# A decoder layer on one core: attention's last periods and the start of the feed forward placed in one order

## What is computed

```
x = x + SelfAttention(LayerNorm(x))        # causal, 16 heads of 64
x = x + CrossAttention(LayerNorm(x), ctx)  # 64 context rows a batch, one head, mask by key
x = x + FFN(LayerNorm(x))
FFN(x): h = silu(x w1 s1) * (x w2 s2); h = gelu(h h1 ..); h = gelu(h h2 ..); h w3 s3
# w1, w2: 256 -> 1024; h1, h2: 1024 -> 1024; w3: 1024 -> 256
```

## Time and profile before

| | us |
|---|---|
| median of 3 runs (lowest to highest) | 1719.96 (1719.22 to 1722.33) |
| the profiled execution | 1718.95 |
| its span, from first to last instruction | 1717.1 |
| PE busy in the span | 1594.4 (93%) |
| DVE busy | 1118.2 (65%) |
| ACT busy | 968.8 (56%) |
| POOL busy | 496.6 (29%) |

### The profile page before, as it was taken

The page is one execution under the profiler, slowest core; times in us unless marked ns, Lnnn a source line. Parts: engine busy times, 40 slices in busy tenths (PEclk is TensorE's granted clock), DMA queues, the critical chain, the costliest instruction groups (busy, mean ns, idle before and its releaser), DMA issues.

```text
span 1717.1 us, 26314 instructions
## 1 busy us (share of the span) xinstructions
PE 1594.4 (93%) x9398; PEld 1332.2 (78%) x9398; DVE 1118.2 (65%) x2733; ACT 968.8 (56%) x2220; POOL 496.6 (29%) x802
## 2 busy tenths in 40 slices
PE   4999999999999999999974489999999899999998
PEld 3788888888888888888863378778888678888887
DVE  5888888888888888888866735665445343333433
ACT  4778777787777877878753334434444342222222
POOL 1444444444444444444440301010001011111110
PEclk9999999999999999999996599999999999999999
DMA  3000000000000000000003312333111352222221
GB/s 135 1 1 1 25 2 26 1 1 26 1 26 1 1 26 2 13 1 2 13 13 138 110 62 75 110 112 111 69 62 44 135 184 75 75 74 74 74 95 41
DMA packets 55470, 87.50 MB, mean 51 GB/s; under 512 B 4128, under 2 KB 33184, under 8 KB 55328
## 3 DMA queue, kind: packets, MB, share of 16 engines
q1 hardware_dynamic: 55328, 85.62, 14.7%
HBM read 56.25 MB, written 29.36 MB: 50 GB/s over the span
## 4 chain that ended last, share of the span: by engine, by line
PE 78%; DVE 11%; ACT 3%; issue 3%; DMA 2%; POOL 2%; SPq 0%; DVEq 0%; ACTq 0%; POOLq 0%
PE bank L913 13%; PE bank L915 11%; PE bank L365 9%; PE bank L380 8%; PE bank L352 7%; PE bank L300 7%; PE bank L302 6%; PE bank L301 6%; PE bank L919 2%; DVE gt L1272 1%; PE bank L1003 1%; DVE Hb L1153 1%; DVE P L606 1%; PE bank L1004 1%; ACT Hb L1048 1%
## 5 line engine op out<-in xcount | busy, mean ns | idle before, releaser
L693 POOL TENSOR_SCALAR P<-P,stats 128x512 f32<-128x512 f32 (+3 forms) x512 | 263.1, 537 | 255.2 <-DVE stats L616 253.6
L470 ACT ACTIVATE P<-P,stats 128x512 f32<-128x512 f32 (+3 forms) x512 | 284.2, 558 | 4.1 <-DVE stats L606 2.0
L521 DVE TENSOR_TENSOR PT<-bank,PT 128x512 fp32r<-128x512 f32 (+1 forms) x384 | 228.8, 596 | 31.7 <-ACT PT L428 31.6
L606 DVE CUSTOM_DVE_ANT_0 P<-bank,cmask 128x384 f32<-128x384 f32 (+3 forms) x512 | 236.2, 481 | 5.6
L428 ACT ACTIVATE PT<-bank 128x512 fp32r<-128x512 f32 (+1 forms) x384 | 194.7, 524 | 66.6 <-PE bank L365 54.1
L1153 DVE TENSOR_TENSOR Hb<-gt,Hb 128x512 fp32r<-128x512 f32 x128 | 91.2, 712 | 212.9 <-ACT Hb L1048 195.1
L913 PE MATMUL bank<-Hb,hw 128*128 128x512 f32 x512 | 206.8, 404 | 6.9 <-POOL flag L1351 4.7
L913 PE MATMUL bank<-w,hw 128*128 128x512 f32 x512 | 203.7, 398 | 3.1 <-DVE w L1153 3.0
L365 PE MATMUL bank<-ident,P 128*128 128x128 f32 x1280 | 190.9, 279 | 6.6 <-DVE PT L521 4.5
L380 PE MATMUL bank<-PT,V 128*128 128x512 f32 (+3 forms) x1024 | 182.8, 321 | 0.0
L380 PEld LDWEIGHTS bank<-PT,V 128*128 128x128 f32 x1024 | 166.8, 188 | 16.1
(11 more groups left out here) (201 smaller groups left out, 3290.3 us busy)
## 6 DMA issues: line engine op xcount, KB each, us to landing
h_scratch<-go SPq DMA_DIRECT2D x64, 256.0 KB, 2.0
xs<-x_scratch SPq DMA_DIRECT2D x24, 512.0 KB, 4.0
qf<-h_scratch SPq DMA_DIRECT2D x32, 256.0 KB, 4.0
pf<-h_scratch SPq DMA_DIRECT2D x32, 256.0 KB, 4.7
stg<-in_h SPq DMA_DIRECT2D x13, 512.0 KB, 3.7
x<-in_x SPq DMA_DIRECT2D x8, 512.0 KB, 4.0
x_scratch<-x SPq DMA_DIRECT2D x8, 512.0 KB, 2.9
x_scratch<-xs SPq DMA_DIRECT2D x8, 512.0 KB, 3.0
```

The lines of the kernel that those rows point to most:

```text
L470: e.activation(p, p, ACT.Exp, bias=st_[:, k:k + 1], scale=-1.0, accum_out=st_[:, 8 + k:9 + k]).then_inc(s_exp, 1)
L521: return e.tensor_tensor(dst, a, b.bitcast(f32), ALU.subtract)
L606: e.tensor_tensor_reduce(P_tile(P, i, a), Sbank(P, i, a)[:, 0:n], cmask[:, 512 - n:512], -1.0, 3.0e38, ALU.add, ALU.min, stats[P % 4][:, k ...
L693: e.tensor_scalar(p, p, stats[P % 4][:, k:k + 1], 1.0, ALU.mult, ALU.mult).then_inc(s_norm, 1)
```

## The change

The two halves become one order. `order()` writes all 68 periods, each engine's period cut in `start`, `mid` and `end`, and puts the early items of the rest between them. `attention_over` is gone. Every tile has a fixed address, those of the rest on top of attention tiles that are dead by then, and each first writer waits on the semaphore of the last reader (`tile_free` and `place_free`, and waits in the items). The item `ln` is cut in `lnsum`, `lnpow`, `lnnorm`; loading a piece (`load`), splitting it (`piece`) and taking its largest value (`big`) are items of their own; there are four staging tiles of 1024 columns in place of six. The splits of `h1` (pieces 10 to 16) and the largest values of pieces 9 to 16 stand between the eight w(0,m), then come `flag 0` and the layer norm of batch 1, which stood ahead of them.

```diff
+def order():
+    between = {
+        (53, 2): [("load", 0), ("load", 1)],
+        (56, 0): [("piece", 0), ("load", 2), ("load", 3), ("load", 4)],
+        (57, 0): [("piece", 1)],
+        (59, 2): [("x1store", 6), ("consts",)],
+        (62, 0): [("piece", 2), ("xload", 0), ("load", 5)],
+        (62, 1): [("piece", 3)],
+        (63, 0): [("xk", 0), ("xk", 1), ("lnsum", 0, 0)],
+        (63, 1): [("mask",), ("bq",), ("piece", 4), ("lnpow", 0, 0), ("lnnorm", 0, 0)],
+        (64, 0): [("xf", 0), ("xf", 1), ("xc",), ("xt", 0, 0), ("load", 6), ("load", 7)],
+        (64, 1): [("piece", 5)],
+        (65, 0): [("pz",), ("xs", 0), ("xv", 0), ("xv", 1), ("xv", 2), ("xv", 3)],
+        (65, 1): [("piece", 6), ("xe", 0), ("load", 8), ("load", 9), ("xload", 1)],
+        (66, 0): [("piece", 7), ("xpt", 0), ("load", 10), ("load", 11)],
+        (66, 1): [("piece", 8), ("xo", 0)],
+        (67, 0): [("piece", 9), ("lnsum", 0, 1), ("lnpow", 0, 1), ("lnnorm", 0, 1)],
+        (67, 1): [("big", 5), ("big", 6), ("xt", 0, 1)],
+    }
+    for p in PERIODS:
+        o += [("start", p)] + between.get((p, 0), []) + [("mid", p)] + between.get((p, 1), [])
+        o += [("end", p)] + between.get((p, 2), [])
+    o += [("big", 7), ("big", 8), ("flag", 2), ("x1store", 7), ("load", 12), ("load", 13), ("load", 14), ("load", 15)]
+    o += [("use", 2), ("load", 16), ("xload", 2)]
...
+    first_h1 = {0: [("piece", 10), ("big", 9)], 1: [("piece", 11), ("big", 10)], 2: [("piece", 12), ("big", 11)],
+                3: [("piece", 13), ("big", 12)], 4: [("piece", 14), ("big", 13)], 5: [("piece", 15), ("big", 14)],
+                6: [("piece", 16), ("big", 15)], 7: [("big", 16), ("flag", 0)] + [(k, 1, 0) for k in ln0]}
...
         for m in range(8):
-            o += [("w", b, m)] + also(b, ("w", m))
+            o += [("w", b, m)] + (first_h1[m] if b == 0 else []) + also(b, ("w", m))
         if b == 0:
-            o += [("flag", 0), ("use", 0)]
+            o.append(("use", 0))
...
-    def attention_over(w):
-
-        w.wait_ge(s_xacc, 8 * B)
-        w.wait_ge(s_x1st[(B - 1) % 2], 16 * ((B + 1) // 2))
...
+    tile_after = {3: (0,), 5: (2, 4), 6: (1, 3), 7: (5,), 8: (6,), 10: (7,), 11: (8,), 13: (9,), 14: (10,), 15: (11,),
+                  16: (12,)}
+    tile_free = {0: ((s_xnT, 2 * B),), 2: ((s_x1st[1], 48),), 6: ((s_xc, 1),), 9: ((s_T, 6 * NP),),
+                 12: ((s_x1st[1], 64),)}
+    place_free = {0: ((s_qk, 2 * 56), (s_v, 56)), 2: ((s_v, NP),), 5: ((s_qk, 2 * NP),), 9: ((s_av, 2 * NP),),
+                  13: ((s_o, NP),)}
...
+            elif kind == "big":
+                src, hi, lo, tile, k, on = pieces[a[0]]
+                w.wait_ge(lo_sem[on], lo_at[a[0]])
+                largest(0, lo.bitcast(f32))
...
+            elif kind == "lnnorm":
...
+                w.wait_ge(s_rstd2, nth["lnsum", b, which] + 1)
+                w.wait_ge(s_x2T, 2 * nth["lnsum", b, which])
+                w.wait_ge(s_S, 4 * (NP - 1))
                 for t in range(NT):
                     i = e.tensor_scalar(xns[:, t, :], x[:, t, :], sm[:, t, 6:7], sm[:, t, 8:9], ALU.subtract, ALU.mult)
                 i.then_inc(s_ln2, 1)
```

More of the change, by code:

```diff
@@ L58, in shared @@
         if kind == "o" and p % 8 == 5 and p // 8 + 1 < B:
-            out += [("xt", p // 8 + 1, 0), ("xt", p // 8 + 1, 1)]
-    return out
[L63 to L79, removed]
+            out += [("rows", p // 8 + 1, 0), ("rows", p // 8 + 1, 1)]
@@ L198, in program @@
[L198 to L203, removed]
-    XWv = sbf(cx, "XWv", [128, 2, 2, 256], f32r)
-    ctr = sbf(cx, "ctr", [128, 2, 2, 512], f32r)
-    more = [sbf(cx, f"stage{i}", [128, 1024]) for i in range(4)]
-    cx.close()
-    Hb = sbf(root, "Hb", [128, 2, 8, 512], f32r)
+    ident = at(0, "ident", [128, 128])
@@ new lines, in program @@
+    half = at(0.5, "half", [128, NT])
+    small = at(0.53125, "lnsmall", [128, NT, 9])
+    stats = [at(0.6875 + 0.09375 * i, f"stats{i}", [128, 24]) for i in range(4)]
+    sm = at(1.0625, "sm0", [128, NT, 9])
+    st = at(1.21875, "st0", [128, 12])
+    flag = [at(1.28125 + 0.03125 * i, f"flag{i}", [128, 2]) for i in range(3)]
+    rmax = [at(1.375 + 0.0625 * i, f"rmax{i}", [128, 16]) for i in range(2)]
+    bqk = at(1.5, "bqk", [128, 2, 2])
+    s1c = at(1.53125, "s1c", [128, 4, 8])
+    L = 1.65625
@@ L402, in pe_attention, with start, mid @@
         project(0, "q")
-        for p in PERIODS:
+        def start(p):
+            pass
+        def mid(p):
             scores(p, 3)
@@ L423, in pe_attention @@
             transposes(p - 1, 1, 2)
+        return {"start": start, "mid": mid, "end": end}
     def act_attention(e, w):
@@ L638, in dve_attention, with start, mid @@
         piece(5)
-        for p in PERIODS:
-            b, q = divmod(p, 8)
-            ahead = b + 1 < B
+        def start(p):
             pt_low(p - 2, 0, 0)
             recip(p - 1, 2)
-            if ahead and q == 6:
-                rows_low(b + 1, 0)
-                rows_low(b + 1, 1)
+            if p % 8 == 6 and p // 8 + 1 < B:
+                rows_low(p // 8 + 1, 0)
+                rows_low(p // 8 + 1, 1)
+        def mid(p):
             pt_low(p - 2, 1, 2)
@@ L660, in dve_attention, with end @@
             y_sum(p - 2, 1)
+        def end(p):
+            b, q = divmod(p, 8)
+            ahead = b + 1 < B
             if ahead and q == 4:
@@ L882, in ln_at @@
     def ln_at(b, which):
-        return 4 * nth["ln", b, which]
+        return 4 * nth["lnsum", b, which]
     def xt_at(b, which):
@@ L1030, in pe_rest @@
                     for t in range(NT):
-                        e.matmul(psum[4 + t][:, 0:256], Hb[:, 0, c, rows[t]], w3[0][:, c, :], start=c == 0, stop=False)
+                        e.matmul(psum[4 + t][:, 0:256], Hb[c][:, 0, rows[t]], w3[0][:, c, :], start=c == 0, stop=False)
                     if c == 7:
@@ L1327, in pool_rest @@
             kind, *a = item
-            if kind == "piece":
+            if kind in steps:
+                steps[kind](a[0])
+            elif kind == "pz":
+                w.wait_ge(s_T, T_P0)
+                for i in range(2):
+                    e.memset(pf[i][:, :, :], 0.0).then_inc(s_pz, 1)
+            elif kind == "piece":
                 src, hi, lo, tile, k, on = pieces[a[0]]
```

355 lines of the change are left out of this document (197 added, 158 removed).

## The result

The changed kernel takes 1722.68 us (median of 12 runs, 1720.12 to 1724.62); the kernel before, run beside it, 1718.95 (1717.08 to 1722.33). The ratio is 1.002, 95% interval 1.0013 to 1.0028: slower by 0.2%, small but clear of the scatter, where I had forecast 1716. The profiled execution took 1721.4, its span 1719.6.

What follows compares the result with a forecast made beforehand. DVE's list was taken to set h(0,0)'s start in PE's hole: 32.4 us early less 13.2 less 16.4 is 2.8, plus 1.0 for PE, 3.8 off 1718.95; plus 1.0 for the median, 1716. Range 1704 to 1726.

Steps and rivals of the forecast that it cites:

- stage 2: The eight w(0,m) with h1 work beside them: 30.7 us to the last `big` against 17.5 before, a cost of 13.2.
- stage 3: Flag 0 and batch 1's layer norm, with POOL changing code each way: h(0,0) 16.4 us behind the last `big`.
- the clock that I gave PE in the drained periods: Before w(0,0): the first ten matmuls of `xf`, `xc` at the lower clock, 8.1 us with transposes and splits.
- POOL's way back behind flag 2: After flag 2's reduction: POOL back by 947.8, 1.3 us after the product of w(0,0).
- Stage 1: Attention's end to the first w(0,0): its product ends at 946.5 instead of 980.15, a benefit of 33.7 us.
- Rival 3: Drained periods: PE falls to the lower clock and stays there, 9 of 12 us showing, 1725; chance 0.2.
- Rival 2: Periods 63 to 67: DVE's pauses take the inserted work, 5 us go, 1711 or less; chance 0.12.
- The POOL term: Beside the eight w(0,m): POOL's four subtractions slow DVE by 2.0 us in all (0 to 4).
- Rival 1: Around flag 0: POOL's code change costs only once, h(0,0) near 985, about 1705; chance 0.2.
- Nothing there is changed: From h(0,0) to the end: PE dense and unchanged, so the time should stay at 718 us.
- Rival 4: Loads in SP's order: new waits deliver no overlap, a landing 4 us late twice, 1722; chance 0.05.
- a warmer start: At h(0,0): PE comes from `xt`, not a pause of 4.67, so part of its slow stretch is over, 1.0 us.

Runs made afterwards that it cites:

- after_warm2: The changed kernel plus 132 extra identity transposes, each block once, ahead of six waits of PE: 1715.19 us (ratio 0.9978).
- clean_beside: The changed kernel with nothing between the parts of periods 63 to 67, the same items following behind 67: 1715.49 us (ratio 0.9991).
- ln_first: The changed kernel with the layer norm of batch 1 ahead of flag 2's last two `big` instead of behind flag 0: 1717.39 us (ratio 0.9991).
- stop_place: The changed kernel's tile addresses with the kernel before's order, stop of all engines included: 1707.34 us (ratio 0.9929 to the kernel before).
- b_gaps: The kernel before plus 288 unused bytes, so w1, w2, hw, XTs and Hb begin alike modulo 256 bytes: 1708.70 us (ratio 0.995).
- after_warm: The changed kernel plus extra identity transposes ahead of seven waits of PE, the blocks in the periods standing twice: 1725.73 us (ratio 1.0034).
- nostop_ahead: The changed kernel with the h1 work and layer norm of batch 1 ahead of the first w(0,0): 1707.62 us (ratio 0.9941).
- clean_ahead_v: The changed kernel, nothing interleaved behind period 62, flag 2 before batch 0's second norm, h1 ahead of w and on DVE: 1700.37 us (ratio 0.9879).
- best_warm: clean_ahead_v plus 229 extra transposes ahead of five waits of PE: 1698.10 us (ratio 0.9883 to the kernel before).

## Why the prediction was wrong, point by point

Of the 16.1 us by which h(0,0) came later than forecast, 10.1 had arisen by flag 2 and 5.0 more by the low part of w(0,0); stage 2 added 1.5 and stage 3 took 0.5 back. The steps that failed are the clock that I gave PE in the drained periods, POOL's way back behind flag 2, the price of POOL's subtractions for DVE, and, with the other sign, the assumption that nothing changes behind h(0,0).

| point | forecast | measured | later by |
|---|---|---|---|
| flag 2 done on DVE | 941.0 | 951.1 | 10.1 |
| w(0,0) begins on PE | 942.0 | 952.45 | 10.4 |
| low part of w(0,0) | 949.1 | 964.2 | 15.1 |
| last `big` | 979.8 | 996.4 | 16.6 |
| h(0,0) | 996.2 | 1012.3 | 16.1 |
| from h(0,0) to the end | 718 | 707.3 | -10.7 |

**Stage 1, the benefit.** My 33.7 us were 22.8 by the product (957.4 instead of 946.5); flag 2 itself came 7.2 later than before (943.8), with more work ahead of it. The step that failed is the clock: I priced only ten matmuls of `xf` at the lower clock. Rival 3 described what happened, with its sign and near enough its size (9). Windows of the changed kernel:

```profile
876.90:882.60 5.70, 5.66 (x29) 5.26 (x29) 3.32 (x10) 2.71 (x7) 2.64 (x5) 0.50 0.00 1
891.00:896.50 5.50, 5.42 (x15) 4.45 (x16) 1.72 (x5) 1.63 (x5) 1.36 (x2) 0.52 0.05 19
913.30:920.00 6.70, 6.70 (x33) 6.70 (x33) 3.53 (x9) 1.25 (x3) 0.00 (x0) 0.51 0.05 17
931.80:937.30 5.50, 5.48 (x24) 5.19 (x24) 2.51 (x3) 1.98 (x2) 0.00 (x0) 0.50 0.90 313
```

These stretches ran at 1.2 GHz, and so did 944 to 947, the transposes shown above. Ahead of them PE had paused for 3.50, 6.18, 1.80, 4.17 and 6.38 us; behind the pause of 1.80 it worked at the higher clock from 911.0 to 913.3 before the clock fell. after_warm2 gives 5.6 us of the 10 to the clock. I took 0.2 for this rival because the clock was 1.00 at 75% busy in the earlier trace rows; but PE's longest pause there was 1.75 us, and the change makes longer ones. Of what is left, the stretches from 877 and from 891 stayed at 0.51 and 0.50 in after_warm2, so their price is still to be added; not interleaving (clean_beside) is worth 3.2 at flag 2, which may overlap with the clock's part; the rest is open. Rival 2, the opposite, is out: clean_beside shows that inserted work pushed attention rather than slipping into its pauses.

**Between flag 2 and the first low part**, 13.1 us instead of 8.1. The product ends 6.3 behind the flag where I had 5.5; the lower clock was in my figure already. POOL comes back at 960.75, 3.35 behind the product, not 1.3 (9.09 of idle time where I took 6.3 from 5.62 and 6.96); and the split takes 2.83 instead of 0.69.

**Stage 2**, 32.2 us instead of 30.7: right in its make-up. The POOL term was too small: I gave the four subtractions 2.0 in all (0 to 4) from one row where a DVE subtraction took 2.27; three splits took 2.15 more each, 6.4, of which one stands in the line above. So this stage holds 4.3 where I had 2.0, and its other terms were 0.8 too high. The Trainium skill, SBUF — State Buffer, section SBUF: two separate sides, says that a DVE instruction with two SBUF inputs and a GpSimd instruction take one pair of ports as an exclusive lock, and that the later of them blocks fully. The trace agrees: the split that starts 0.05 behind POOL's subtraction ends 0.55 behind its end. An estimate by that rule, with POOL's whole 2.33 for each of the three splits, would have been 7.0 instead of 2.

**Stage 3**, 15.8 instead of 16.4: right, and ln_first shows it by its causes, as the wait from flag to h(0,0) falls to 5.1 when the power is taken out from behind the reduction. Rival 1 (a code change only once) is out.

**The rest.** "Nothing there is changed" was the worst step: the changed places of the tiles, not the order, made the matmuls behind h(0,0) faster (stop_place, b_gaps). I looked at which instructions follow h(0,0), saw the same ones, and did not ask if their operands lay elsewhere, though the change moves every tile. It gave back 10.7 of the 16.1, so that the total missed the forecast by only 6.7: luck, since no term of the prediction had it. The prediction did name the sign: it would be wrong as a whole if the time from h(0,0) to the end did not stay at 718. Rival 4 (loads late) did not show: ACT waited for two loads up to flag 2, 0.62 and 0.26 us.

**The sum.** I had 996.2 and 717.1 for the rest (718.1 less 1.0 for a warmer start, which can't be made out: h(0,0) took 0.78 as before). 16.1 later and 9.8 shorter is 6.3 above my 1715.2 for the profiled execution: 1721.5, measured 1721.4. The median stood 1.3 above that, not 1.0. Three slips in the working don't touch the forecast: by the share of 826 to 855, DVE's work in the 22 us ahead of 876.90 is 18 us, not 17; from 855 to 998.97 it is 144 us, not 143; and rival 4, twice 4 us on 1716, is 1724, not 1722.

## What to carry to other kernels

When an edit moves tiles, ask if their starts changed relative to each other. Look at the pace of the matmuls far from the edit, and try starts of the loaded weights and the moving rows that are alike modulo 256 bytes; 288 bytes of gaps gave this kernel 0.5%. Work put between the short bursts of a draining pipeline cost twice here, by its own time and by the clock that PE lost in the pauses. A POOL reduction is priced with both changes of code, and what stands behind it on POOL, and who waits for that, decides if they cost nothing or 15 us.

## What the runs showed of the hardware

- Matmuls of 128x512 at the higher clock follow each other in 227 to 228 ns (mean of the two hidden layers) where both operands begin alike modulo 256 bytes, and in 233 where they differ by 32 or 128 bytes. Six in a row of the changed kernel, second hidden layer:

```profile
1500.32 0.39 PE L980 MATMUL bank<-w,hw 128*128 128x512 f32 x1
1500.54 0.39 PE L978 MATMUL bank<-w,hw 128*128 128x512 f32 x1
1500.77 0.39 PE L980 MATMUL bank<-w,hw 128*128 128x512 f32 x1
1501.00 0.39 PE L978 MATMUL bank<-w,hw 128*128 128x512 f32 x1
1501.22 0.39 PE L980 MATMUL bank<-w,hw 128*128 128x512 f32 x1
1501.45 0.39 PE L978 MATMUL bank<-w,hw 128*128 128x512 f32 x1
```

and of the kernel before at the same time:

```profile
1500.33 0.40 PE L913 MATMUL bank<-w,hw 128*128 128x512 f32 x1
1500.57 0.40 PE L915 MATMUL bank<-w,hw 128*128 128x512 f32 x1
1500.80 0.39 PE L913 MATMUL bank<-w,hw 128*128 128x512 f32 x1
1501.03 0.39 PE L915 MATMUL bank<-w,hw 128*128 128x512 f32 x1
1501.26 0.39 PE L913 MATMUL bank<-w,hw 128*128 128x512 f32 x1
1501.49 0.39 PE L915 MATMUL bank<-w,hw 128*128 128x512 f32 x1
```

  Five steps take 1.13 us above and 1.16 below. Why, the runs do not tell.
- POOL's way back from the reduction took 6.7 to 7.3 us in most runs, but 9.09 in the changed kernel, 8.39 to 8.96 in after_warm, after_warm2 and nostop_ahead, and 10.35 and 10.32 in clean_ahead_v and best_warm, all behind flag 2. In each of those long pauses the DMA engines carried loads, 1.05 MB in the four of 8.39 to 9.09 and 2.6 MB in the two over 10, and in the short ones of clean_beside and ln_first next to nothing; but the kernel before carried 1.49 MB in its pause of 6.96, most of it from 2 us into the pause on. So the loads that flag 2 lets go are a likely cause, which no run tested.
- 132 transposes that compute nothing, laid into PE's waits, brought h(0,0) of the changed kernel 5.8 us forward in the profile, and its time from 1722.68 (ratio 1.002) to 1715.19 (0.9978).
